# Keys of the cross attention made for four heads at a time: one token tile against 512 weight columns

## The reference, cut to what matters

```
q = rmsnorm((x_norm @ Wq).reshape(B, Sq, 16, 128), gq)
k = rmsnorm((ctx @ Wk).reshape(B, Skv, 16, 128), gk)      # Wk is 128 x 2048
v = (ctx @ Wv).reshape(B, Skv, 16, 128)
out = softmax(q k^T / sqrt(128)) v, heads joined, @ Wo
```

## Time and profile before

| | |
|---|---|
| median of three runs | 1162.65 us |
| the profiled execution, its own time | 1166.83 us |
| its span | 1165.0 us |
| TensorE busy | 994.8 us (85%) |
| VectorE, ScalarE, GpSimd busy | 745.4 us, 648.9 us, 515.7 us |
| stage F0, from its first work to the next stage's | 193.9 us to 258.7 us |
| stage A1 | 258.7 us to 602.9 us |
| one step of A1 in its middle | 9.66 us |

### The profile page before, as it was taken

One profiled execution on the slowest core, in us unless ns is written; L12 is line 12 of the kernel. 1 busy time (PEld: TensorE's weight loads), 2 busy tenths in 40 slices (PEclk: granted clock), 3 DMA queues, 4 the chain that ended last, 5 costly groups with the idle time before them and its releaser, 6 DMA issues.

```text
span 1165.0 us, 15796 instructions
## 1 busy us (share of the span) xinstructions
PE 994.8 (85%) x5573; PEld 802.6 (69%) x5576; DVE 745.4 (64%) x1308; ACT 648.9 (56%) x1261; POOL 515.7 (44%) x513
## 2 busy tenths in 40 slices
PE   5367675557999999999978899988999999999898
PEld 1022232236899998899867788866878888778787
DVE  6799997964555555555526565577565675667575
ACT  3845456674766666677633566723656644343443
POOL 0266550023666666566533344343443544344352
PEclk7579887887999999999989999999999999899999
DMA  9100100007000000000022000000000220000000
GB/s 340 45 1 0 54 1 0 1 23 301 1 1 2 1 1 2 1 2 1 1 105 95 1 1 1 1 1 1 1 1 1 107 97 1 1 1 1 9 11 19
DMA packets 4734, 35.84 MB, mean 31 GB/s; under 512 B 1160, under 2 KB 2192, under 8 KB 3152
## 3 DMA queue, kind: packets, MB, share of 16 engines
q1 hardware_dynamic: 4656, 34.83, 7.7%
HBM read 33.78 MB, written 1.05 MB: 30 GB/s over the span
## 4 chain that ended last, share of the span: by engine, by line
PE 52%; DVE 15%; ACT 6%; issue 5%; DVEq 0%; POOL 0%; ACTq 0%; POOLq 0%
PE psum L377 13%; PE psum L379 12%; PE psum L378 12%; PE psum L604 4%; DVE f_h_lo L1512 4%; PE psum L592 2%; ACT f_silu L1030 2%; PE psum L547 2%; DVE f_silu L1495 2%; DVE x_norm L1072 2%; PE psum L551 1%; DVE f_silu L1504 1%; PE psum L668 1%; PE psum L703 1%; ACT a_P L946 1%
## 5 line engine op out<-in xcount | busy, mean ns | idle before, releaser
L377 PE MATMUL psum<-x_norm_T_hi,f_wgu_hi 128*128 128x512 f32 x400 | 177.7, 444 | 0.0
L1504 DVE TENSOR_TENSOR f_silu<-f_silu,psum 128x512 f32<-128x512 f32 x100 | 68.7, 687 | 165.9 <-ACT f_silu L1030 165.9
L379 PE MATMUL psum<-x_norm_T_hi,f_wgu_lo 128*128 128x512 f32 x400 | 161.2, 403 | 0.0
L378 PE MATMUL psum<-x_norm_T_lo,f_wgu_hi 128*128 128x512 f32 x400 | 160.8, 402 | 0.0
L749 ACT ACTIVATE f_h_hi<-f_silu 128x512 fp32r<-128x512 f32 x100 | 63.0, 630 | 173.1 <-DVE f_silu L1495 172.6
L377 PE MATMUL psum<-f_wd_hi,f_h_hi 128*128 128x256 f32 x400 | 121.7, 304 | 13.2 <-DVE f_h_lo L1512 13.1
L1512 DVE TENSOR_TENSOR f_h_lo<-f_silu,f_h_hi 128x512 fp32r<-128x512 f32 x100 | 123.6, 1236 | 3.6 <-ACT f_h_hi L749 3.5
L1581 POOL TENSOR_TENSOR f_wgu_lo<-f_wa,f_wgu_hi 128x512 fp32r<-128x512 f32 x44 | 56.6, 1286 | 144.7 <-ACT f_wgu_hi L749 144.6
L378 PE MATMUL psum<-f_wd_lo,f_h_hi 128*128 128x256 f32 x400 | 114.2, 285 | 0.0
L379 PE MATMUL psum<-f_wd_hi,f_h_lo 128*128 128x256 f32 x400 | 113.9, 285 | 0.0
L1653 POOL TENSOR_TENSOR m_dBu<-m_du,m_Bs 128x1024 f32<-128x1024 f32 x32 | 77.0, 2409 | 67.6 <-DVE m_du L1170 21.7
(11 more groups left out here) (297 smaller groups left out, 2706.1 us busy)
## 6 DMA issues: line engine op xcount, KB each, us to landing
f_wa<-in_f1a SPq DMA_DIRECT2D x1, 8448.0 KB, 25.2
f_w<-in_f3w SPq DMA_DIRECT2D x1, 5376.0 KB, 17.5
w_raw<-in_w0raw SPq DMA_DIRECT2D x1, 3072.0 KB, 16.4
f_w<-in_f2w SPq DMA_DIRECT2D x1, 3072.0 KB, 14.5
f_wb<-in_f1b SPq DMA_DIRECT2D x1, 2304.0 KB, 8.2
a_wo<-in_wo SPq DMA_DIRECT2D x2, 1024.0 KB, 12.3
a_wq<-in_wq SPq DMA_DIRECT2D x1, 2048.0 KB, 25.0
x_res<-in_x SPq DMA_DIRECT2D x1, 1024.0 KB, 7.3
```

The costliest lines, as they stand in the source:

```text
L377: mm(out, wh, xh, start=start, stop=False, **kw)
L378: mm(out, wh, xl, start=False, stop=False, **kw)
L379: return mm(out, wl, xh, start=False, stop=stop, **kw)
L1504: V.tensor_tensor(sg[g % 2][:, :], sg[g % 2][:, :], ps[:, 3 + 2 * (g % 2), :], ALU.mult).then_inc(S("f_m"), 1)
```

## The change

- One unit of key work is now one token tile (128 tokens) against 512 weight columns, which are four heads: 3 matmuls of 512 columns in place of 12 of 128. Step 0 makes four units at once (the four token tiles of heads 0 to 3) into banks 2 to 5, and every later step one unit, of a group of four heads further on, until step 28; the last three steps make no keys (`KB` = 29).
- Squares, sums, scaling and transposes have the same size for each step as before, save in step 0, where they are four times as wide (two instructions of 1024 columns each, and 16 columns for GpSimd's power). The scaled keys go to two buffers of four heads each.
- Wk is split whole (2048 columns), ahead of the stage; `parts(i)` splits only Wq. In F0 ScalarE does the split of the context, of Wk and of heads 0 and 1 of Wq before `inputs(0)` in place of at t = 6, and GpSimd does its four subtractions before its first `rstd_of` of the stage. The low part of Wk takes the place of Wk itself.
- The first key unit of A1 no longer waits for the transposed input (`xT_ready`).
- `f1a` is 14 tiles, `f1b` 14.

```diff
-    J1A = 22
+    J1A = 14
+    at["WK"] = at["A1"]
+    rks0, rk0 = (place("W1", f"a_{n}0", [P, 4 * TH]) for n in ("k_sum", "rk"))
+    KB = HEADS2 - TH + 1
+    ktok = [place("B1a", f"a_k_tok{i}", [P, TH, 4, P]) for i in range(2)]
+    wkh = place("B1a", "a_wk_hi", [P, HEADS * P], f32r)
+    wkl = place("WK", "a_wk_lo", [P, HEADS * P], f32r)
-    AQ = KC * P + P
+    AQ = KC * P
@@ TensorE, attn1
-            pe.wait_ge(S("xT_ready"), 1)
             pe.wait_ge(S("a_ctx"), 1)
+            pe.wait_ge(S("a_wk"), 1)
+            def keys(i):
+                units = range(TH) if i == 0 else (i + TH - 1,)
+                for n in units:
+                    g, t = n // TH, n % TH
+                    sl = slice((g // 4) * HALF + t * P, (g // 4) * HALF + (t + 1) * P)
+                    wsl = slice((g % 4) * HALF, (g % 4 + 1) * HALF)
+                    last = mm3(ps[:, 2 + t if i == 0 else 7, :], ch[:, sl], cl[:, sl], wkh[:, wsl], wkl[:, wsl], True, True)
+                last.then_inc(S("a_k"), 1)
             def keys_queries(i):
+                if i == 0:
+                    keys(0)
+                    pe.wait_ge(S("xT_ready"), 1)
+                elif i < KB:
+                    pe.wait_ge(S("a_kT"), i)
+                    keys(i)
                 pe.wait_ge(S("a_w"), i + 1)
-                if i:
-                    pe.wait_ge(S("a_kT"), i)
-                for t in range(TH):
-                    ...
-                    last = mm3(ps[:, 7, ksl], ch[:, sl], cl[:, sl], hi[:, KC * P:AQ], lo[:, KC * P:AQ], True, True)
@@ ScalarE, ffn0
+            copy(ch[:, :], ctxT[:, :]).then_inc(S("a_ch"), 1)
+            loaded(act, "wq", "wk")
+            copy(wkh[:, :], wk[:, :]).then_inc(S("a_wkh"), 1)
+            parts(0)
+            parts(1)
             inputs(0)
...
-                if t == NT - 2:
-                    copy(ch[:, :], ctxT[:, :]).then_inc(S("a_ch"), 1)
-                    loaded(act, "wq", "wk")
-                    parts(0)
-                    parts(1)
@@ ScalarE, squares, step 0
+                if i == 0:
+                    for b in range(2):
+                        last = A(Pm[b][:, :, :], ps[:, 2 + 2 * b:4 + 2 * b, :], ACT.Square)
+                    last.then_inc(S("a_ksq"), 1)
@@ VectorE, step 0 (key_norms, keys_scaled)
+                        last = V.tensor_reduce(rks0[:, 8 * b:8 * b + 8], Pm[b][:, :, :]..., AX, ALU.add)
...
+                        last = V.tensor_tensor(ktok[0][:, 2 * b:2 * b + 2, :, :]..., ps[:, 2 + 2 * b:4 + 2 * b, :]..., bc(rk0...), ALU.mult)
@@ GpSimd
+        def key_weights_lo():
+            pool.wait_ge(S("a_wkh"), 1)
+            G.tensor_tensor(wkl[:, :], wk[:, :], wkh[:, :].bitcast(f32), ALU.subtract).then_inc(S("a_wk"), 1)
...
             if s == "F0":
-                rstd_of()
                 context_lo()
+                key_weights_lo()
                 parts(0)
                 parts(1)
+                rstd_of()
                 rstd_of()
```

More of the change, by code:

```diff
@@ L548, in norm_transpose @@
                 last.then_inc(S("a_qn"), 1)
-                pe.wait_ge(S("a_ktok"), i + 1)
+                pe.wait_ge(S("a_ktok"), min(i + 1, KB))
+                if i >= KB:
+                    pe.wait_ge(S("a_kT"), i)
                 for t in range(TH):
-                    last = nc.tensor.transpose(ps[:, 7, t * P:(t + 1) * P], ktok[:, t * P:(t + 1) * P], ident[:, :])
+                    last = nc.tensor.transpose(ps[:, 7, t * P:(t + 1) * P], ktok[i // 4 % 2][:, t, i % 4, :], ident[:, :])
                 last.then_inc(S("a_kt"), 1)
@@ L755, in parts @@
                 act.wait_ge(S("a_w"), i - 1)
-            copy(awh[i % 2][:, 0:KC * P].rearrange("p (c n) -> p c n", c=KC), wq[:, :, (i % HEADS) * P:(i % HEADS + 1) * P])
-            copy(awh[i % 2][:, KC * P:AQ], wk[:, (i % HEADS) * P:(i % HEADS + 1) * P]).then_inc(S("a_wh"), 1)
+            copy(awh[i % 2][:, :].rearrange("p (c n) -> p c n", c=KC), wq[:, :, (i % HEADS) * P:(i % HEADS + 1) * P]).then_inc(S("a_wh"), 1)
         def norm_T(n, banks, dst):
@@ L894, in squares @@
             def squares(i):
-                act.wait_ge(S("a_k"), i + 1)
+                if i < KB:
+                    act.wait_ge(S("a_k"), i + 1)
                 if i:
                     act.wait_ge(S("a_qn"), i)
-                A(ksq[:, :], ps[:, 7, :], ACT.Square).then_inc(S("a_ksq"), 1)
+                if i == 0:
+                    for b in range(2):
+                        last = A(Pm[b][:, :, :], ps[:, 2 + 2 * b:4 + 2 * b, :], ACT.Square)
+                    last.then_inc(S("a_ksq"), 1)
+                elif i < KB:
+                    A(ksq[:, :], ps[:, 7, :], ACT.Square).then_inc(S("a_ksq"), 1)
                 act.wait_ge(S("a_q"), i + 1)
-                act.wait_ge(S("a_rks"), i + 1)
+                act.wait_ge(S("a_rks"), min(i + 1, KB))
                 A(qsq[:, :], ps[:, 6, :], ACT.Square).then_inc(S("a_qsq"), 1)
@@ L1298, in key_norms @@
                     dve.wait_ge(S("a_rk"), i)
-                V.tensor_reduce(rks[:, :], ksq[:, :].rearrange("p (t d) -> p t d", t=TH), AX, ALU.add).then_inc(S("a_rks"), 1)
+                if i == 0:
+                    for b in range(2):
+                        last = V.tensor_reduce(rks0[:, 8 * b:8 * b + 8], Pm[b][:, :, :].rearrange("p t (c d) -> p (t c) d", c=2), AX, ALU.add)
+                    last.then_inc(S("a_rks"), 1)
+                else:
+                    V.tensor_reduce(rks[:, :], ksq[:, :].rearrange("p (n d) -> p n d", n=4), AX, ALU.add).then_inc(S("a_rks"), 1)
             def queries_lo(i):
@@ L1306, in keys_scaled @@
                 dve.wait_ge(S("a_rk"), i + 1)
[L1307 to L1310, removed]
+                if i == 0:
+                    for b in range(2):
+                        last = V.tensor_tensor(ktok[0][:, 2 * b:2 * b + 2, :, :].rearrange("p t n d -> p (t n) d"),
+                                               ps[:, 2 + 2 * b:4 + 2 * b, :].rearrange("p t (n d) -> p (t n) d", n=4),
+                                               bc(rk0[:, 8 * b:8 * b + 8].unsqueeze(2), [P, 8, P]), ALU.mult)
+                    last.then_inc(S("a_ktok"), 1)
+                else:
+                    g, t = (i + TH - 1) // TH, (i + TH - 1) % TH
+                    if g >= 2:
+                        dve.wait_ge(S("a_kt"), 4 * (g - 1))
+                    V.tensor_tensor(ktok[g % 2][:, t, :, :], ps[:, 7, :].rearrange("p (n d) -> p n d", n=4),
+                                    bc(rk[:, :].unsqueeze(2), [P, 4, P]), ALU.mult).then_inc(S("a_ktok"), 1)
             def query_norms(i):
@@ L1334, in attn1 @@
                     ac_lo(i - 2)
+                if i + 1 < KB:
+                    key_norms(i + 1)
                 if i + 1 < HEADS2:
-                    key_norms(i + 1)
                     queries_lo(i + 1)
+                if i + 1 < KB:
                     keys_scaled(i + 1)
@@ L1546, in parts @@
             pool.wait_ge(S("a_wh"), i + 1)
[L1547 to L1550, removed]
+            G.tensor_tensor(awl[i % 2][:, :].rearrange("p (c n) -> p c n", c=KC), wq[:, :, (i % HEADS) * P:(i % HEADS + 1) * P],
+                            awh[i % 2][:, :].bitcast(f32).rearrange("p (c n) -> p c n", c=KC), ALU.subtract).then_inc(S("a_w"), 1)
         def context_lo():
@@ L1615, in _ @@
                 for i in range(HEADS2 + 1):
-                    if i + 1 < HEADS2:
+                    if i + 1 < KB:
                         norms(i + 1)
@@ L1747 @@
         "wvT0": wvT[:, :8], "wvT1": wvT[:, 8:], "wo0": wo[:, :8], "wo1": wo[:, 8:],
-        "f1a": f1w[:, :22], "f1b": f1w[:, 22:],
+        "f1a": f1w[:, :14], "f1b": f1w[:, 14:],
         "f1r": router(np.concatenate([f["L1_ffn_gate_w"], f["L1_ffn_shared_gate_vec"]])),
```

9 lines of the change are left out of this document (3 added, 6 removed).

## The result

| | median of its runs | kernel before, same chip | ratio, 95% interval |
|---|---|---|---|
| after the change | 1166.15 us (14 runs, 1163.43 to 1169.19) | 1162.11 us (14 runs) | 1.0037 [1.0022, 1.0051] |

The change makes the kernel slower by 0.37%, some 4.3 us (2.6 to 5.9). The forecast was +2.8 us on 1162.65, 1165.5, and slower was given 0.55.

The account below looks back on a forecast made before the run. TensorE was taken to bound A1's steps, with a second chain only 0.20 us behind. Terms -5.0 - 2.0 + 7.7 + 2.1 = +2.8 us on 1162.65 gave 1165.5 us, slower; 8-in-10 range 1157.5 to 1169.5.

Parts of the forecast that it names:

- Steps of A1: Keys against 512 columns save TensorE 0.64 us a step, of which 0.20 is kept in 25 steps: 5.0 us gained.
- 0.20 us of slack: In A1's steps the chain through the low part of attention times context is only 0.20 us behind TensorE.
- R2: Rival: A1 is bound by TensorE alone and takes the whole 0.64 us, -16.0 us, 1154.5; chance 0.05.
- the other chain: A1: output product, scores, key transposes, exponentials, low part, back to TensorE; 9.46 us, nothing in it shortened by the change.
- Start of F0: VectorE in `quantise_x` takes turns with GpSimd's moved subtractions, so the stage starts 7.7 us late; bounds 0 and 8.5.
- R1: Rival: smaller collision at F0's start, 2.3 us or none in place of 7.7, 1160.1 or 1157.8; chance 0.23.
- Splits out of t = 6: Tile t = 6 of F0: five ScalarE copies leave, 1.96 us come off the stage; bounds 0 to 2.5.
- Start of A1: Step 0's fourfold squares, sums, power and scaling delay the first copy of transposed keys; costs 2.1 us, 0.9 to 3.2.
- Loads and the small copies: The larger `f1b` load is hidden by 60 us, and Wk's per-step copy and subtraction lie off A1's chain: nothing.
- R3: Rival: one or two more clock drops in A1's steps 18 to 20, power dear, 1168 to 1169.5; chance 0.2.
- R4: Rival: TensorE's 0.44 us stand in each A1 step lowers the clock repeatedly, 1200 us or more; chance 0.02.

Follow-up runs that it names:

- the first experiment: Changed kernel, but GpSimd begins its four subtractions of stage F0 only when VectorE has quantised the first input: 1159.95 us, ratio 0.9977.
- the last experiment: Changed kernel, but its splits, Wk's too, are back at t = 6 of F0 as in the kernel before: 1163.89 us, ratio 1.0001.

## Why the prediction was right

- **Steps of A1: -5.0, measured -4.76.** The step of 9.46 us is 9.47; TensorE waits in 31 steps. The bound read from two pairs of rows, 0.20 us of slack, holds, though TensorE was busy in 134.85 of 137 us. The keys save 0.56 us, not 0.64: a 512-column matmul took 0.80/3 = 0.27 us here and not 0.24; the first of the three is the slow one (0.50 us, where the first query matmul takes 0.39). It changed nothing, since only 0.20 could be kept (9.66 - 9.47 = 0.19). R2 was wrong as to the kernel as changed and right as to TensorE: with the other chain out of the way the step is 8.93, a little below the 9.0 that R2 gave.
- **Start of F0: +7.7, measured +7.06.** The mechanism and its place are as written. I had put the first scaling or the four of 256 columns behind the subtractions; it was the small scalings L1248 and L1250, on 128x4, that took the two full waits. The size was 0.6 us too large: Wk's subtraction took 4.50 us and not 4.65, and the two parts of Wq cost VectorE 1.1 us together. The reciprocal between the two scalings ran undisturbed (0.18 us), and Wk's subtraction, begun at 196.32, was ahead of L1250 (196.64). The Trainium skill's SBUF — State Buffer, section "SBUF: two separate sides", has the port pair of VectorE and GpSimd as an exclusive lock under which the loser waits for the whole instruction; the trace agrees on both sides: L1250 ended 0.02 us after Wk's subtraction, and in the first experiment GpSimd's context subtraction took 3.38 us in place of 2.35, beside a VectorE instruction of 1.23 us on 128x2048. R1 fell with this, and the first experiment shows what no collision would have given: 0.9977, 1159.95 us.
- **Splits out of t = 6: -2.0, measured -1.0.** This is the term that was mis-sized most. ScalarE's 1.96 us are gone: the two groups of matmuls there are 4.37 us apart, as forecast, where they were 6.32 apart. But in the last tiles TensorE ran at half its clock for longer than before. Timeline of TensorE after, the last tiles of F0:

```profile
248.18 1.05 PE L494 MATMUL psum<-w_quant,q_hqT 128*128 128x256 bf16 x8 [1.15 <-ACT q_hqT L765]
...
252.55 1.42 PE L494 MATMUL psum<-w_quant,q_hqT 128*128 128x256 bf16 x8 [2.88 <-ACT q_hqT L765]
...
255.94 1.89 PE L494 MATMUL psum<-w_quant,q_hqT 128*128 128x256 bf16 x8 [1.12 <-ACT q_hqT L765]
```

  in the kernel before

```profile
249.10 1.89 PE L489 MATMUL psum<-w_quant,q_hqT 128*128 128x256 bf16 x8 [1.81 <-ACT q_hqT L749]
```

  and in the first experiment

```profile
243.75 1.89 PE L494 MATMUL psum<-w_quant,q_hqT 128*128 128x256 bf16 x8 [2.88 <-ACT q_hqT L765]
...
247.61 1.05 PE L494 MATMUL psum<-w_quant,q_hqT 128*128 128x256 bf16 x8 [1.12 <-ACT q_hqT L765]
```

  The eight matmuls take 1.05 us at full clock and 1.89 at half. In the kernel before the tile at t = 6 was late, two groups were slow (1.71 and 1.89 us at 244.73 and 249.10), and the clock was back for the last two. In the kernel after the granted clock was 0.50 from 256.0 to 263.7, up to the end of the stage. From the group at 248.18 (244.73 before) to A1's first transpose it is 15.58 us in place of 13.97, so 1.61 of the 1.95 us are lost again; another 0.67 us were gained between `q_xT` and tile 5, for which I have no cause. The stand of 2.88 us ahead of the group at 252.55 does not decide it alone: the first experiment has the same stand, only one slow group, and again 13.97 us, and its stretch from `q_xT` is 57.60 us, 1.4 below before. Of the seven kernels with the splits at the start of F0 four have 13.97 us there and three 15.4 to 15.6; what sets how long the clock stays low no run shows.
- **Start of A1: +2.1 (0.9 to 3.2), measured +1.8** to the first `a_AC_lo`, +2.8 to the first `keys_hi`, of which the next key unit gives 1.0 back, as forecast (1.45 us from its start to the first query matmul, where it was 2.59). The power over 16 columns took 2.89 us, nearer the dear end (3.3) than the cheap one (1.0), 0.7 us above the middle that I took. That the sum fits is luck in part: the four key units ended 5.3 us after the first transpose and not 6.6.
- **Loads and the small copies: 0, measured 0.** R3, one or two more drops of the clock in steps 18 to 20, was not seen. There is one low stretch, as before. By stretches (granted clock last but two) it is in the kernel after

```profile
480.00:490.00 10.00, 9.74 (x58) 9.16 (x59) 4.38 (x8) 5.59 (x15) 3.83 (x6) 0.83 0.00 0
```

  and before it was 0.85 from 470 to 480 and 0.98 from 480 to 490. The distances between the low parts there (10.43, 11.06, 11.91, 11.00 us) are those of before (10.61, 11.07, 11.92, 10.95). Nor did the short stand in each step lower the clock (1.00 over 137 us), which rules out R4.

The sum came nearer than its terms: 0.6 us too much loss at the start of F0, 0.3 too much at the start of A1, against 1.0 too much gain at t = 6 and 0.2 in the steps, nearly cancel, which is luck. The direction does not hang on it: with the whole 2.0 us at t = 6 the four stretches would still sum to +2.1.

What stays open: the runs say +4.3 us and the four stretches of the ledger +3.1. Of the 1.2 us between them 0.4 lie outside the span: the time is 2.18 to 2.26 us longer than the span in all 14 runs after, and 1.75 to 1.86 in the 43 runs before that have both. The runs give no cause for that. The rest is inside the interval (2.6 to 5.9), and the ledger has one execution of each kernel, in which chance counts: the last tiles of F0 differ by 1.6 us with the clock alone, and the start of F0, ahead of everything that the kernels change, lies between 190.0 and 193.9 us in the ten profiled executions.

## What to carry to other kernels

A busy share of 98% does not make TensorE the only bound: measure, in two steps of which one was late, how far the next chain is behind, and count only that much of a saving, or first move the waiting block behind one that needs nothing new (here the move is worth 5.7 us of A1 alone and 22.1 with the saving in place; both together are 26.9). Work moved into an idle stretch of GpSimd is not free if VectorE is on the path there: each of its long instructions can hold one VectorE instruction for nearly its full length, even one of 128x4 elements (2.06 of 2.35 us, 3.97 of 4.50), so start it by the signal of VectorE's last critical instruction.

## What the runs showed that I had not expected

- Which VectorE instructions stand behind GpSimd: TENSOR_SCALAR with fp32 input did (128x4: 0.17 to 2.23 us and 0.23 to 4.20 us; 128x256; 128x1024: 0.69 to 2.65 us). Undisturbed beside a GpSimd subtraction were the reciprocal of 128x4 (0.18 us), a TENSOR_SCALAR of a single column, 128x1 (0.15 us at 240.06, in the last experiment), and the SCALAR_TENSOR_TENSOR of 128x256 that reads PSUM (0.47 us at 246.14 there, while GpSimd was at its parts of Wq).
- GpSimd's power costs 1.01, 2.26 and 2.89 us for 128x4, 128x12 and 128x16, 0.157 us for each further column; the multiply-add on the same 128x16 takes 0.21 us.
